# Operand loads of an attention and expert layer: a new layout in DRAM, a later row of ones, new due steps

## What is computed

```python
xn = _layernorm(x, axis=-1)
x = x + attn(xn, Wq, bq, Wk, bk, Wv, bv, Wo, bo) + ffn(xn, Wr, Wg, Wu, Wd)
# attn: q, k, v = xn W + b; probs = softmax(q k^T * scale + causal); y = probs v; y Wo + bo
# ffn: the 2 best of xn Wr, their softmax as weights w_e; sum over e of w_e * ((silu(xn Wg[e]) * (xn Wu[e])) Wd[e])
```

## Time and profile before

| | |
|---|---|
| median of 3 runs | 440.68 us |
| profiled execution | 442.84 us, span of its instructions 441.0 us |
| busy | PE 403.7, VectorE 334.5, ScalarE 220.7, GpSimd 196.0 us |
| mean granted TensorE clock | 0.959 |
| packets of DMA | 42,116, 71.68 MB; of these SP's queue 28,778 and 27.08 MB |

### The profile page before, as it was taken

One profiled execution on the slowest core, in us unless ns is written; L12 is line 12 of the kernel. 1 busy time (PEld: TensorE's weight loads), 2 busy tenths in 40 slices (PEclk: granted clock), 3 DMA queues, 4 the chain that ended last, 5 costly groups with the idle time before them and its releaser, 6 DMA issues.

```text
span 441.0 us, 8403 instructions
## 1 busy us (share of the span) xinstructions
PE 403.7 (92%) x2755; PEld 224.9 (51%) x2755; DVE 334.5 (76%) x1043; ACT 220.7 (50%) x511; POOL 196.0 (44%) x224
## 2 busy tenths in 40 slices
PE   8599959896999799999999999999999999999993
PEld 8266523354425533654566556654655466455332
DVE  6453999899779559876767795688488889881795
ACT  1173434242563377277545345464656444457970
POOL 6241125664335661765388236534654346313320
PEclk9799986899899999999999999999999999999996
DMA  8529853777327831594199144945495335200782
GB/s 247 87 91 253 278 174 115 238 237 244 107 62 210 223 135 46 187 271 144 24 273 311 51 146 148 272 123 178 146 256 134 124 133 151 92 14 3 242 261 71
DMA packets 42116, 71.68 MB, mean 163 GB/s; under 512 B 7479, under 2 KB 32184, under 8 KB 42074
## 3 DMA queue, kind: packets, MB, share of 16 engines
q0 software_dynamic: 9360, 39.99, 28.2%
q1 hardware_dynamic: 28778, 27.08, 21.9%
q10 hardware_dynamic: 3936, 4.08, 3.5%
HBM read 55.85 MB, written 15.60 MB: 162 GB/s over the span
## 4 chain that ended last, share of the span: by engine, by line
PE 62%; DVE 21%; DMA 6%; issue 4%; ACT 4%; POOL 2%; SPq 0%; ACTq 0%; POOLq 0%; DVEq 0%
PE psum L1373 13%; PE psum L1336 11%; PE psum L1316 10%; PE psum L1382 8%; DVE psum L1016 6%; PE psum L1293 6%; PE psum L1222 6%; PE psum L1246 3%; ACT probs L930 3%; DVE mxa L1019 3%; PE psum L1355 3%; DMA bqk<-in_bqk 2%; DVE x L1072 2%; PE psum L1363 1%; DMA xg<-xn_rows,token 1%
## 5 line engine op out<-in xcount | busy, mean ns | idle before, releaser
L930 ACT ACTIVATE probs<-psum 128x512 f32<-128x512 f32 (+1 forms) x320 | 150.7, 579 | 56.6 <-PE psum L1316 54.5
L1016 DVE CUSTOM_DVE_ANT_0 psum<-psum,maskrow 128x384 f32<-128x384 f32 (+3 forms) x256 | 116.5, 526 | 11.5 <-PE psum L1293 11.2
L1316 PE MATMUL psum<-packq,packk 99*128 99x512 bf16 (+7 forms) x384 | 88.2, 339 | 9.5 <-ACT probs L930 2.7
L1019 DVE TENSOR_REDUCE mxa<-psum 128x1 f32<-128x512 f32 x128 | 80.3, 681 | 16.6 <-PE psum L1293 16.2
L1336 PE MATMUL psum<-probs,v 128*32 128x512 f32 (+3 forms) x768 | 77.8, 503 | 1.1 <-POOL probs L856 1.0
L856 POOL TENSOR_SCALAR_AFFINE_SELECT probs<-probs 128x512 f32<-128x512 f32 (+1 forms) x48 | 41.0, 855 | 59.0 <-ACT probs L930 58.7
L1316 PEld LDWEIGHTS psum<-packq,packk 99*128 99x128 bf16 (+1 forms) x384 | 31.3, 98 | 68.5 <-issue 23.4
L823 POOL DMA_INDIRECT xg<-xn_rows,token x39 | 37.7, 966 | 40.1 <-PE psum L1363 33.1
L841 POOL DMA_INDIRECT expert_rows<-wvr,slots x39 | 39.4, 1009 | 36.0 <-ACT wvr L950 24.2
L1293 PE MATMUL psum<-packk,packq 48*128 48x512 bf16 (+3 forms) x384 | 48.3, 328 | 3.9 <-DVE mxa L1019 2.6
L1373 PE MATMUL psum<-xgt,wexp 128*128 128x128 f32 x384 | 48.0, 278 | 0.6 <-issue 0.6
(11 more groups left out here) (121 smaller groups left out, 463.0 us busy)
## 6 DMA issues: line engine op xcount, KB each, us to landing
qk_parts<-stage SPq DMA_DIRECT2D x24, 256.0 KB, 3.1
stage<-expert_rows SPq DMA_DIRECT2D x16, 256.0 KB, 4.1
packq<-qk_parts SPq DMA_DIRECT2D x32, 96.0 KB, 4.6
packk<-qk_parts SPq DMA_DIRECT2D x28, 96.0 KB, 5.2
x<-in_x SPq DMA_DIRECT2D x4, 512.0 KB, 5.6
packq<-qk_parts SPq DMA_DIRECT2D x32, 64.0 KB
xn_rows<-probs ACTq DMA_DIRECT2D x4, 512.0 KB, 5.4
out<-x SPq DMA_DIRECT2D x16, 128.0 KB, 2.2
```

Of the source, the lines that this page charges most:

```text
L930: act.activation(probs[:, g % RING, h, 0:width], psum[:, bank, 0:width], ACT.Exp, scale=SCALE)\
L1016: ins = dve.tensor_tensor_reduce(out=chunk, in0=chunk, in1=maskrow[:, BANK - width:], scale=1.0, scalar=NEG, op0=ALU.add, op1=ALU.max, acc ...
L1019: ins = dve.tensor_reduce(into, chunk, op=ALU.max, axis=AX.X)
L1316: ins = pe.matmul(psum[:, bank, at:at + width], packk[0:KROWS[h // UP], h // UP, u % SLOTS, j // HALF, h % UP, P * (j % HALF):P * (j % HAL ...
```

## The change

Four things are changed. (1) `spread_ones` waits for four "lo" steps instead of none, and its job depends on the fourth instead of the first. (2) `qk_d` has the chunk of 512 tokens as an own dimension ahead of the row, so that the two heads of a load lie together: a piece of a load is 2 KB instead of 1 KB. The source of a load is written `r d (h t)`, its destination `p (h t)`. (3) The loads of units 3 to 7 wait each for a step of its own, `step_before_load`: 0, 1, 3, 4, 6 and 7 steps after the step for which all of them waited. (4) The planner adds `TILED` (96 ns) where TensorE goes between tilings of kinds "c" or "r" and others, and `SETTLE` (3 ns) otherwise, in place of a table; a probs x v step counts 45 ns more and a down product 860 instead of 853 ns.

```diff
--- before.py
+++ after.py
@@ -65,6 +65,7 @@
          for js in [*((j,) for j in range((c + 1) * BANK // P - 2)), ((c + 1) * BANK // P - 2, (c + 1) * BANK // P - 1)]]
 NS = len(STEPS)
 HALF = TB // 2
+LOAD_EVERY = 3
 GROUPS = [[(0, 0, 0), (0, 2, 0)], [(0, 3, 0)], [(0, 1, 0), (1, 1, 0)], [(1, 0, 0), (1, 2, 0)], [(1, 3, 0)]]
 EARLY = len(GROUPS)
 GROUPS += [[(p, i, 0)] for p in range(UP) for i in range(HALF, TB)] + [[(p, 7, 1)] for p in range(UP)]\
@@ -102,6 +103,11 @@
 def diagonal(n):
     c, js = STEPS[n]
     return P * js[0] >= BANK * c
+
+
+def step_before_load(u, c, r):
+
+    return NS * (u - SLOTS + 1) - 1 + (c * len(RUNS) + r) * LOAD_EVERY // 2
 
 
 def last_of_half(n):
@@ -235,7 +241,7 @@
                 held[take[0]] = held.get(take[0], 0) + 1
                 bank_of[take] = bank
             if engine == "PE":
-                at += SWITCH.get((mode, own), 20)
+                at += TILED if own != mode and {own, mode} & {"c", "r"} else SETTLE
                 mode = own
             end = at + ns
             free_at[engine] = end
@@ -258,9 +264,8 @@
         return order, bank_of
 
 
-SWITCH = {("r", "r"): 8, ("b", "r"): 105, ("f", "r"): 105, ("c", "r"): 105, ("r", "b"): 105, ("r", "f"): 105, ("r", "c"): 105,
-          ("b", "b"): 5, ("f", "f"): 15, ("b", "f"): 95, ("f", "b"): 20, ("b", "c"): 105, ("f", "c"): 105,
-          ("c", "b"): 110, ("c", "f"): 120}
+TILED = 96
+SETTLE = 3
 STAY = 8000
 NEG_LAG = 8000
 SPREAD = 0.6
@@ -294,7 +299,7 @@
 
     for n, (ns, due) in enumerate(((1100, -30), (2000, 30), (1800, 31))):
         job("POOL", ("const", n), ns, due=due)
-    job("SP", ("ones",), 1500, [("POOL", ("const", 1)), ("POOL", ("lo", 0))], due=2000, lag=2000, size=400000)
+    job("SP", ("ones",), 1500, [("POOL", ("const", 1)), ("POOL", ("lo", QKS // 4 - 1))], due=2000, lag=2000, size=400000)
     for q in range(4):
         job("SP", ("x", q), 500, lag=2000, due=-10, size=524288)
     job("ACT", ("weights_qk",), 950, [("SP", ("x", 1))], due=-50, lag=2000, size=540000)
@@ -357,11 +362,11 @@
     for u in range(UNITS):
         b, g = divmod(u, G)
         for c in range(2):
-            after = [("SP", ("store", 4 * b + 2 * (g // 2) + c))]
-            if u >= SLOTS:
-                after += [("PE", ("s", NS * (u - SLOTS + 1) - 1, UH - 1))]
             due = 8 + 10 * c if u == 0 else 60000 + c if u == 1 else nat_due(u, 0) - 30000 + c
             for r in range(len(RUNS)):
+                after = [("SP", ("store", 4 * b + 2 * (g // 2) + c))]
+                if u >= SLOTS:
+                    after += [("PE", ("s", step_before_load(u, c, r), UH - 1))]
                 job("SP", ("load", u, c, r), 1800 if u else 960, after, due, lag=2500 if u else 4500, size=131072)
                 if u == 0:
                     job("ACT", ("load", u, c, r), 960, after, due, lag=4500, size=131072)
@@ -403,7 +408,7 @@
         if diagonal(n):
             job("POOL", ("mask", g), 700, after, due)
             after = [("POOL", ("mask", g))]
-        pe(("pv", g), width * 4 / 2.4, after + ([("ACT", ("v", TB * (u // G + 1) - 1))] if n == 0 and u % G == 0 else []), due_at[g + 1] - 100,
+        pe(("pv", g), width * 4 / 2.4 + 45, after + ([("ACT", ("v", TB * (u // G + 1) - 1))] if n == 0 and u % G == 0 else []), due_at[g + 1] - 100,
            ("y", u, c) if js[0] == 0 else None, "c")
         if last_of_half(n):
             due = due_at[g + 1]
@@ -445,7 +450,7 @@
         pe(("gu", i), 1850, [("ACT", ("xgt", i)), ("POOL", ("fetch", i))], due + 500, ("gu", i))
         job("ACT", ("tanh", i), 280, [("PE", ("gu", i))] + ([("DVE", ("hid", i - 2))] if i >= 2 else []), due + 1000)
         dve(("hid", i), 780, [("ACT", ("tanh", i))] + ([] if i else [("DVE", ("bias",))]) + ([("PE", ("d", i - 2))] if i >= 2 else []), due + 1000, ("gu", i))
-        pe(("d", i), 853, [("DVE", ("hid", i))], due + 2000, ("d", i))
+        pe(("d", i), 860, [("DVE", ("hid", i))], due + 2000, ("d", i))
         job("ACT", ("yo", i), 280, [("PE", ("d", i))] + ([("POOL", ("scatter", i - 2))] if i >= 2 else []), due + 2000,
             frees=("d", i))
         job("POOL", ("scatter", i), 1300, [("ACT", ("yo", i))], due + 2000, lag=1800)
@@ -495,7 +500,7 @@
 
 
         xn_d = nc.dram_tensor("xn_rows", [N, D], F32).ap()
-        qk_d = nc.dram_tensor("qk_parts", [2, 2, PARTS, HD, H // 2, N], BF16).ap()
+        qk_d = nc.dram_tensor("qk_parts", [2, 2, PARTS, N // BANK, HD, H // 2, BANK], BF16).ap()
         z_d = nc.dram_tensor("expert_rows", [2 * N, D], F32).ap()
 
 
@@ -687,6 +692,7 @@
 
             def spread_ones():
                 sp.wait_ge(consts, 2)
+                sp.wait_ge(qk_lo, QKS // 4)
                 for k, last in ((0, SHIFT[0] + PARTS), (1, GAP[1])):
                     sp.dma_start(packk[SHIFT[k]:last, k, :, :, :, :].rearrange("p s c h t -> p (s c) (h t)"),
                                  ones_row[SHIFT[k]:last, :].unsqueeze(1).to_broadcast([last - SHIFT[k], 2 * SLOTS, UP * BANK]))\
@@ -703,8 +709,7 @@
                 for part in (1, 0, 2):
                     if part == 0:
                         sp.wait_ge(qk_lo, 2 * w + 2)
-                    cols = slice(T * b + BANK * n, T * b + BANK * (n + 1))
-                    sp.dma_start(qk_d[:, grp, part, :, :, cols].rearrange("o d h t -> (d h) o t"),
+                    sp.dma_start(qk_d[:, grp, part, T // BANK * b + n, :, :, :].rearrange("o d h t -> (d h) o t"),
                                  stage[:, w % 2, part, :].rearrange("p (o t) -> p o t", o=2)).then_inc(qk_out[w % 2], 16)
 
             def load(u, c, r):
@@ -712,16 +717,15 @@
                 b, g = divmod(u, G)
                 grp, h0 = divmod(UH * g, H // 2)
                 if u >= SLOTS:
-                    wait_filled(sp, ("s", NS * (u - SLOTS + 1) - 1, UH - 1))
+                    wait_filled(sp, ("s", step_before_load(u, c, r), UH - 1))
                 sp.wait_ge(qk_out[c], 16 * PARTS * (2 * b + grp + 1))
                 rows, *first, length = RUNS[r]
                 landed = (lead_in if r < LEADS else rest_in)[u % SLOTS][c]
                 for k in range(2):
                     for op, pack in enumerate((packq, packk) if u else (packq,)):
-                        src = qk_d[op, grp, first[op]:first[op] + length, :, h0 + UP * k:h0 + UP * (k + 1),
-                                   T * b + BANK * c:T * b + BANK * (c + 1)]
-                        sp.dma_start(pack[rows[k]:rows[k] + HD * length, k, u % SLOTS, c, :, :],
-                                     src.rearrange("r d h t -> (r d) h t")).then_inc(landed, 16)
+                        src = qk_d[op, grp, first[op]:first[op] + length, T // BANK * b + c, :, h0 + UP * k:h0 + UP * (k + 1), :]
+                        sp.dma_start(pack[rows[k]:rows[k] + HD * length, k, u % SLOTS, c, :, :].rearrange("p h t -> p (h t)"),
+                                     src.rearrange("r d h t -> r d (h t)")).then_inc(landed, 16)
 
             def neg_rows(x):
 
@@ -883,9 +887,9 @@
                 act.wait_ge(qk_out[c], 16 * PARTS)
                 rows, _, first, length = RUNS[r]
                 for k in range(2):
-                    src = qk_d[1, 0, first:first + length, :, UP * k:UP * (k + 1), BANK * c:BANK * (c + 1)]
-                    act.dma_start(packk[rows[k]:rows[k] + HD * length, k, 0, c, :, :],
-                                  src.rearrange("r d h t -> (r d) h t")).then_inc((lead_in if r < LEADS else rest_in)[0][c], 16)
+                    src = qk_d[1, 0, first:first + length, c, :, UP * k:UP * (k + 1), :]
+                    act.dma_start(packk[rows[k]:rows[k] + HD * length, k, 0, c, :, :].rearrange("p h t -> p (h t)"),
+                                  src.rearrange("r d h t -> r d (h t)")).then_inc((lead_in if r < LEADS else rest_in)[0][c], 16)
 
             def copy_xnt(q, c):
                 bank = wait_filled(act, ("xnt", q, c))
```

## The result

The changed kernel took 482.9 us (median of 4 runs, 481.17 to 484.47), the kernel before 440.05 beside it: a ratio of 1.0975, interval 1.0913 to 1.1037. It is 42.9 us slower. The forecast was 462, 21 us slower, with 437 to 488 as range: the sign and the cause were right, the size was half of what came. The time lies inside the range, but above the 448 to 478 us that rival C, the forecast's own mechanism, was given.

What follows compares the result with a forecast made beforehand. PE was taken as nearly full from 133 us, with slack earlier. 442.8 + 19 (start and narrow loads) + 3 (later loads) - 1 (planner) = 463.8, less 2.2 for the profiled execution: 461.7, predicted 462, range 437 to 488.

Steps and rivals of the forecast that it cites:

- rival C: Whole kernel: the forecast's own case, narrow loads delaying the first scores; 448 to 478 us, chance 56%.
- Part 1: Start: without the ones ahead, bqk lands when the transposes end and the clock stays fast; gain 0 to 7.4, 7 taken.
- rival A: Loads: they run on 16 engines as before, or on changing ones, so nothing is late; 432 us, chance 15%.
- rival B: Loads: narrow but cheap packets, or unit 1's loads fall behind the maxima; 434 to 450 us, likely 443, chance 13%.
- Part 2, few engines: Loads from DRAM: those of two and three parts run on 2 and 3 engines, the same first ones; net +19 us.
- Price of a packet: Loads: a 2 KB packet costs 94 ns, twice the 1 KB price, with bounds 47 and 106.
- The maxima: Unit 0: negated maxima land at 85 us behind 528 packets on the first engine, so scores begin 22 us later.
- What comes back after it: After the first scores: two VectorE waits of 1.39 us come back, little more, leaving net +19 us.
- Part 3 and the steady stretch: Units 3 to 7: first engine near full, 208 of 201 us, costs 4; spreading the loads wins 1; +3 us.
- Part 4: Planner costs: only the order of instructions changes; -2 to +3 us, -1 taken.
- Rival D: Later loads: at 106 ns an excess of 23 us reaches PE as late operands or gathers; 478 to 500 us, 16%.
- The signs: Profile after: first product near 12.5 us at 1.00 clock, DMA share near 3/16, 96 KB loads landing well over 8 us.

Runs made afterwards that it cites:

- e1: The kernel before with one change, the rows of ones issued behind four "lo" steps; 439.35 us against 440.46, ratio 1.0015.
- e3: The changed kernel with the chunk ahead of the part in DRAM, so part and row merge (16 engines, 2 KB pieces); 440.84 us, ratio 1.0052.
- e6: The changed kernel with narrow loads only in the second batch, units 4 to 7, and merged rows in units 0 to 3; 446.03 us, ratio 1.0133.
- e11: e8 with all loads of a unit waiting for the same step again; 432.52 us, ratio 0.9824.
- e8: e3 with the loads of unit 1 made to stand behind the negated maxima of unit 0 on SP; 432.72 us against 440.95, ratio 0.9813.
- e12: e8 with the planner's old switch table and old costs; 434.77 us, ratio 0.9866.

## Why the prediction was right, and where its size was off

**Part 1 (+7 us taken).** Right at the start: the first products at 13.39 us and 4.53 us long, against 16.96 and 7.44, are 6.5 us won. Wrong in what became of them. The sum carried the 7 us on to the end in rival A and B. In e1 PE then waits 4.4 us for the negated maxima, and nothing of the 7 us can be measured in the time. What failed is the cost of the rows of ones in their new place: I named the first reader of the loads as the one who waits, and not the maxima, which stand further back on the same queue. The ones are 2.7 of the 5.7 us that the maxima lose there, slower issues of the loads the rest. What then takes the remaining gain is open.

**Part 2, few engines.** Right. The packet counts give 2 and 3 engines exactly; what was forecast as "about 6,100 packets fewer" should by the prediction's own counts have been 7,380, and that is what came. The windows of after show it too. From 50 to 52 us no compute engine works at all, and the share of DMA is 0.15, between 2 and 3 of 16, though beside 30 packets of SP's queue 37 of ScalarE's move; from 88 to 101 us, when SP's queue is alone, it is 0.19, that is 3 of 16, the loads on 16 engines among them:

```profile
50.00:52.00 2.00, 0.00 (x0) 0.00 (x0) 0.00 (x0) 0.00 (x0) 0.00 (x0) 0.50 0.15 57
...
88.00:101.00 13.00, 12.34 (x86) 4.55 (x85) 3.49 (x10) 5.69 (x12) 4.70 (x5) 0.66 0.19 67
```

That also answers what no row of before showed, whether narrow transfers that follow each other take the same engines. In these 13 us SP issues 19 loads, four of them of one part (16 pieces outermost, so on 16 engines; the share is 0.37 from 94 to 96 us, just behind their issue), and the others on 2 or 3. If they took changing engines and ran side by side, each would be done some 1.5 us (16 x 0.092) after its issue, two of them would be under way at a time, and 4 to 6 engines busy, a share near 0.3; between 90 and 92 us it is 0.13, that is 2 of 16. If a queue moved one whole transfer after the other, whatever its engines, the loads of one part issued from 92.81 us on would have to wait for the eight narrow ones issued from 87.08 on, 11.8 us of work; but the share rises with their issue. What is left is that the narrow transfers share the same engines. Rival A falls, and e3 shows the 440.84 us that it would have given, not the 432 that I had worked out.

The Trainium skill (DMA: Bandwidth & Descriptors, Why a DMA increments its semaphore by 16 and not by 1) says that a transfer issued by SP or ScalarE takes the lowest-numbered engines, the largest number up to 16 that divides the slowest dimension of both sides. The counts of 2 and 3 and the shares of 0.13 and 0.19 agree; the numbers of the engines themselves no view here shows.

**Price of a packet (94 ns taken).** The same 13 us give it: all packets, and those of SP's queue.

```profile
DMA packets 509, 0.87 MB, mean 67 GB/s; under 512 B 87, under 2 KB 87, under 8 KB 508
...
q1 hardware_dynamic: 508, 0.86, 18.7%
```

16 x 13 us x 0.187 over the 421 packets of 2 KB are 92 ns, if the 87 small ones cost nothing, and 83 ns if each costs as much as one of 1 KB. A piece of 2 KB costs 1.8 to 2 times one of 1 KB (47 ns). The loads of unit 1 were also still ahead of the maxima, so both conditions of rival B fall.

**The maxima (85 us forecast, scores 22 us later).** They were in at 86.4 and the scores came 23.7 us later, so the sum of 528 packets gives the right time for this point. How it comes about is different in one thing. The sum has the maxima issued in time and waiting behind packets; in the trace SP issues without a pause from 27.74 to 82.26 us, the loads of units 0 and 1 end at 73.5 instead of 52.5 in e3, the maxima are issued only from 77.70 on, and the last lands 4 us after its issue. The backlog on the engines reached them as issues that took longer.

**What comes back after it (3 us taken): the step that failed.** Nothing came back. From the first scores to unit 1 the kernel before needs 85.3 us (148.06 less 62.78) and the changed one 89.5. I had priced the backlog only as a delay of what PE waits for first. It costs in three more places.

First, the engines that issue. SP's issue of a load, mostly 0.42 to 0.46 us before and 1.35 at most, takes up to 3.25 us in the backlog, and ScalarE's issue of the 512 KB copy of xn took 9.09 us. The timeline of SP and of ScalarE after:

```profile
49.12 3.25 SPq L727 DMA_DIRECT2D packq<-qk_parts  x1
```

```profile
44.94 9.09 ACTq L882 DMA_DIRECT2D xn_rows<-probs  x1
54.07 0.37 ACT L919 COPY v<-psum 128x256 f32<-128x256 f32 x1 [8.46 <-issue]
```

ScalarE computes nothing during this issue: its copy of v stands 8.46 us, and PE the 8.41 for lg that are on its list. In the kernel before the first two of the four copies took 0.39 and 0.42 us to issue and the other two 1.51 together, and ScalarE's longest stand for an issue was 2.60 us. The copies have 128 rows outermost; they landed in 11.7 us in the median instead of 5.4, one of them in 23.5. This is the same transfer that the sum had counted only as "0 to 6, I take 3" us of work on the first engine: its price on the queue that issues it was left out.

Second, the stores. They use all 16 engines, and stand behind the loads of unit 1 and then of unit 2: in SP's order, and on the first engines. ScalarE can't reuse `stage` until they are out (timeline of ScalarE, the list of its waits, and timeline of SP after):

```profile
85.38 1.27 ACT L906 ACTIVATE stage<-psum,bqk 128x512 bf16<-128x512 f32 x2 [17.24 <-DMA qk_parts<-stage]
```

```profile
ACT stage L906 <- DMA qk_parts<-stage: 26.0, 2, 17.2
```

```profile
102.43 25.60 SPq L712 DMA_DIRECT2D qk_parts<-stage  x9
```

The first row waits for the store that SP issues from 73.56 us on, behind the loads of unit 1. The nine issues in the row of SP begin at 81.89 before and span 15.66 us. They now begin 20.5 us later and span 25.60. The first takes 6.77 us to issue, where before none took over 0.55; one that is issued at 112.1 us lands at 121.4, where before none took over 5.7 us to land; and on it hang ScalarE's second wait, 8.75 us until 121.49, then VectorE's remainder and PE's 3.65 us at 123 us. Gathers and fetches move at that time too, so not all of the store's delay need be the narrow loads'. Beside it the first gather waits 4.46 us.

Third, the clock. The forecast said that the clock falls in the stall and charged nothing. After PE stood for 14.01 us it was granted 0.50, the 1.2 GHz level, for some 8 us of nearly full work, until 96 us:

```profile
88.00:90.00 2.00, 1.80 (x4) 0.32 (x3) 1.40 (x3) 1.69 (x4) 0.46 (x1) 0.50 0.10 32
90.00:92.00 2.00, 1.81 (x7) 0.48 (x6) 0.00 (x0) 1.79 (x5) 0.48 (x2) 0.50 0.13 44
...
94.00:96.00 2.00, 2.00 (x16) 0.67 (x12) 0.00 (x0) 0.31 (x1) 2.00 (x2) 0.50 0.37 125
```

In the 8 us from 88 to 96 PE is busy 7.34 us (1.73 of them from 92 to 94); that would have been 3.7 at full clock if the products had followed each other as closely. Over the whole span PE is busy 8.5 us longer for the same products, though part 1 alone makes it 2.5 us less (401.2 in e1). So 8.5 of the 38.6 us are products that run longer, and 30.1 are standing.

**Part 3 and the steady stretch (+3 taken; bounds 0 to 15 less 0 to 3).** The sum found the first engine full (208 of 201 us) and took 4 us of it. From unit 1 (+27.9) to the end (+38.6) it was 10.7 us, within the bounds and over three times the 3 taken. Not all of it is lateness in this stretch: from the first scores of unit 1 to those of unit 4 PE runs 928 products where it ran 912, busy 127.1 us instead of 122.5, so up to 4.6 us of it is work put off from the start. e6 shows 5.2 in batch 1, as gathers that are late five times. Of the spreading nothing can be measured (e11 against e8).

**Part 4 (-1 taken, -2 to +3).** e12 against e8 gives -2 by the medians, with intervals that overlap.

**Rival D (478 to 500, 16%).** The time fell in its range, but not by its mechanism: it said that the excess of the later loads over 201 us reaches PE, as late operands or late gathers. At most 10.7 of 38.6 us are of that kind. The loss is at the start, as in the forecast, and larger. That the range up to 488 holds the measured time is owed to the room that was given to D, and is luck as far as the mechanism goes.

**The signs.** The first product came at 13.39 instead of 12.5 us, at a granted clock of 1.00. The share of DMA is 0.20 from 64 to 72 us, near 3 of 16, but 0.43 from 79 us to the first scores, when stores move too. No view has the landing times of the 96 KB loads. From unit 1 on PE has no wait for operands.

Summed up: 19 taken for the first stretch, 27.9 measured; 3 less 1 taken for the rest, 10.7 measured; together 21 against 38.6. The step that failed is the first: what a backlog costs beyond the wait for the maxima. The medians are 42.9 apart, 4.3 more: the profiled execution of before (442.84) lay 2.8 us above the 440.05 of this comparison, that of after (481.34) 1.6 below its median.

## What to carry over

Before changing the source of a transfer, write down the outermost dimension of both sides after merging: if it is 2 or 3, the transfer runs on 2 or 3 engines, and in this case always on the same ones. A backlog on these engines has to be charged to everything that passes through them: the later transfers on all 16 engines, the engine that issues them, for as long as the issue hangs, and TensorE's clock after the stall. When a gain at the start doesn't reach the end, follow the delay from unit to unit before naming a cause: here one dependence more, with the merged layout and the other parts kept, turned 440.84 into 432.72 us, and most of it was won far behind the wait that it took away.

## What the runs showed of the hardware that was not expected

An issue of a transfer is not a fixed price: 0.42 us for a load on SP behind little else, 3.25 us at 49.12 us of after, 9.09 us for one copy of 512 KB on ScalarE. Even before a backlog has built up a narrow load costs more to issue than one on 16 engines, 0.60 to 0.79 us against 0.42 (the timeline of SP after: a load of 1 part, on 16 engines, one of 2, one of 3). It is not the longer piece: in e3 the loads of two and three parts, with the same 2 KB pieces on 16 engines, take 0.42 us to issue.

```profile
86.61 0.42 SPq L727 DMA_DIRECT2D packk<-qk_parts  x1
87.08 0.67 SPq L727 DMA_DIRECT2D packq<-qk_parts  x1
...
89.76 0.71 SPq L727 DMA_DIRECT2D packq<-qk_parts  x1
```

And a copy of 512 KB whose packets go to 16 engines is late beside narrow loads of another engine's queue: 11.7 us to land in the median where it was 5.4, one 23.5, with some 13 engines idle for much of the time (a share of 0.20 from 42 to 44 us, 0.15 and 0.13 from 50 to 54, 0.21 and 0.19 from 56 to 60). Whether the issue hangs because a queue of the first engines is full, or for another reason, no view shows.
